# Layer 1 of a two-layer graph attention kernel: another order of the blocks per row, and of the steps that make the parts of the probabilities

## What is computed

```python
q, k, v = (split_heads(h @ W) for W in (Wq, Wk, Wv))
sim = jnp.einsum('bhid,bhjd->bhij', q, k) * scale
sim = jnp.where(adjacency_mask[:, None, :, :], sim, neg)
attn = jax.nn.softmax(sim, axis=-1)
out = jnp.einsum('bhij,bhjd->bhid', attn, v)
return out.transpose(0, 2, 1, 3).reshape(...) @ Wo + bo
```

## Time and profile before

| | |
|---|---|
| median of 3 runs | 2656.8 us |
| the profiled execution | 2656.29 us, span 2654.5 us |
| TensorE, matmuls busy | 2587.7 us (97%) |
| VectorE busy | 1990.9 us (75%) |
| ScalarE busy | 1754.5 us (66%) |
| GpSimd busy | 1399.6 us (53%) |
| mean granted TensorE clock | 0.994 |
| q, k and v blocks of layer 1, share of the chain that ended last | 19% |

### The profile page before, as it was taken

The page is one execution under the profiler, slowest core; times in us unless marked ns, Lnnn a source line. Parts: engine busy times, 40 slices in busy tenths (PEclk is TensorE's granted clock), DMA queues, the critical chain, the costliest instruction groups (busy, mean ns, idle before and its releaser), DMA issues. The chain is left out here.

```text
span 2654.5 us, 62516 instructions
## 1 busy us (share of the span) xinstructions
PE 2587.7 (97%) x20882; PEld 1393.6 (52%) x20886; DVE 1990.9 (75%) x6361; ACT 1754.5 (66%) x5020; POOL 1399.6 (53%) x2790
## 2 busy tenths in 40 slices
PE   6999999999999999999999999997999999999998
PEld 3455555555555555555555555554555555555554
DVE  6477778777877777777777777786777777777766
ACT  3566666666666666666666666675777777777774
POOL 4255545545554555555555555544565656555552
PEclk9999999999999999999999999998999999999999
DMA  5367766776667666766776677678786777778774
GB/s 141 61 136 158 144 135 133 149 155 130 145 141 140 145 128 144 149 142 133 141 147 141 131 140 146 148 141 195 158 175 160 169 163 170 164 160 170 158 149 102
DMA packets 945489, 387.43 MB, mean 146 GB/s; under 512 B 857617, under 2 KB 859153, under 8 KB 945169
## 3 DMA queue, kind: packets, MB, share of 16 engines
q1 hardware_dynamic: 945168, 383.44, 69.0%
HBM read 114.86 MB, written 67.11 MB: 69 GB/s over the span
## 5 line engine op out<-in xcount | busy, mean ns | idle before, releaser
L552 ACT ACTIVATE probs<-probs,negmax 128x128 f32<-128x128 f32 x1024 | 398.2, 390 | 455.6 <-DVE negmax L124 455.6
L465 POOL TENSOR_TENSOR o_sb<-o_sb,xres 128x512 f32<-128x512 f32 x127 | 161.5, 1272 | 496.5 <-DVE o_sb L739 493.1
L166 PE MATMUL l_ps_pj<-hT,room 128*128 128x512 f16 x1488 | 346.7, 383 | 2.3 <-ACT room L1343 2.3
L166 PE MATMUL ps_pj<-wm_hi,hT 128*128 128x512 f16 x1024 | 326.4, 380 | 12.6 <-DVE wm_lo L761 6.8
L166 PE MATMUL ps_pj<-wv_hi,hT 128*128 128x512 f16 x1024 | 326.4, 380 | 0.0
L166 PE MATMUL ps_pj<-hT,wk_hi 128*128 128x512 f16 x1024 | 305.9, 380 | 0.0
L166 PE MATMUL ps_pj<-hT,wq_hi 128*128 128x512 f16 x1024 | 304.5, 379 | 0.0
L1357 ACT ACTIVATE l_probs<-l_probs,l_negmax 128x128 f32<-128x128 f32 x512 | 199.2, 390 | 139.0 <-DVE l_negmax L124 138.8
L1292 POOL TENSOR_TENSOR l_h<-l_h 128x512 f16<-128x512 f32 x120 | 139.6, 1164 | 282.3 <-DVE l_out_sb L1440 245.0
L124 DVE CUSTOM_DVE_ANT_0 probs<-ps_sc,mask 128x128 f32<-128x128 f32 x1024 | 235.4, 285 | 47.4 <-PE ps_sc L981 46.7
L721 DVE SCALAR_TENSOR_TENSOR c<-cprobs,c 128x512 f16<-128x512 f32 x256 | 185.2, 723 | 79.6 <-ACT c L559 79.2
(11 more groups left out here) (172 smaller groups left out, 6198.8 us busy)
## 6 DMA issues: line engine op xcount, KB each, us to landing
xg<-in_x SPq DMA_DIRECT2D x128, 256.0 KB, 3.4
xres<-in_x SPq DMA_DIRECT2D x128, 256.0 KB, 3.1
x_scratch<-o_sb SPq DMA_DIRECT2D x128, 256.0 KB, 2.4
out<-l_out_sb SPq DMA_DIRECT2D x128, 256.0 KB, 3.3
l_ring<-x_scratch SPq DMA_DIRECT2D x124, 256.0 KB, 3.2
mask_u<-in_adj SPq DMA_DIRECT2D x64, 64.0 KB, 2.8
cpT<-c SPq DMA_TRANSPOSE x256, 3.2
xg<-x_scratch SPq DMA_DIRECT2D x12, 256.0 KB, 3.2
```

The costliest lines, as they stand in the source:

```text
L166: last = pe.matmul(out, a(kt), b(kt), start=(n == 0), stop=(n == 3 * kts - 1))
L465: nc.gpsimd.tensor_tensor(o_sb[:, j % 2], o_sb[:, j % 2], xres[:, j % 2], ALU.add).then_inc(res_done, 1)
L552: last = nc.scalar.activation(probs[:, i], probs[:, i], ACT.Exp, bias=negmax[:, u % 2, i:i + 1], scale=-1.0, accum_out=zsum[:, u % 4, hh:h ...
```

## The change

TensorE's order in an iteration becomes project_qk(n+4), project_v(n+4), project_out(n-4), scores(n+1), weigh_values(n-2). ScalarE and VectorE make the parts of the probabilities of row n at the start of iteration n, where before they made those of row n+1 at the end of it. On ScalarE v_high goes ahead of exps and behind relu and h_high; on VectorE v_low goes to the front, behind p_low. `normalise(n)` gets a wait for p_low(n-1), since it overwrites what that reads. At the start of the layer relu and h_high of rows 8 and 9 no longer stand behind p_high(0). The queues of GpSimd and SP stay as they are.

```diff
--- before.py
+++ after.py
@@ -1370,25 +1370,25 @@
                                      scale=1.0 / F16_SCALE).then_inc(ahi_done, 1)
 
             exps(0)
-            p_high(0)
             relu(MADE)
             h_high(MADE)
             relu(MADE + 1)
             h_high(MADE + 1)
             for n in range(B - QUAD):
                 qk_copy(n + QUAD)
+                p_high(n)
                 if n + 10 < B:
                     relu(n + 10)
                     h_high(n + 10)
+                v_high(n + QUAD)
                 exps(n + 1)
-                v_high(n + QUAD)
                 if n >= 2:
                     aT_high(n - 2)
-                p_high(n + 1)
             for n in range(B - QUAD, B - 1):
+                p_high(n)
                 exps(n + 1)
-                p_high(n + 1)
                 aT_high(n - 2)
+            p_high(B - 1)
             for i in range(B - 3, B):
                 aT_high(i)
 
@@ -1417,6 +1417,7 @@
 
             def normalise(n):
                 dve.wait_ge(exp_done, count(n + 1))
+                dve.wait_ge(plo_done, count(n))
                 nc.vector.reciprocal(rec[:], zsum[:, n % 2]).then_inc(rec_done, 1)
                 dve.wait_ge(rec_done, count(n + 1))
                 nc.vector.tensor_tensor(nprobs[:], probs[:], rec[:].unsqueeze(2).to_broadcast([P, HB, P]),
@@ -1442,28 +1443,28 @@
 
             row_max(0)
             normalise(0)
-            p_low(0)
             for i in range(HELD, 15):
                 stats(i)
             for n in range(B - QUAD):
+                p_low(n)
+                v_low(n + QUAD)
                 if n >= 4:
                     add_residual(n - 4)
                 row_max(n + 1)
                 if n + 15 < B:
                     stats(n + 15)
                 normalise(n + 1)
-                v_low(n + QUAD)
                 if n >= 2:
                     aT_low(n - 2)
-                p_low(n + 1)
             row_max(B - 3)
             for n in range(B - QUAD, B - 1):
+                p_low(n)
                 add_residual(n - 4)
                 normalise(n + 1)
                 if n + 2 < B:
                     row_max(n + 2)
-                p_low(n + 1)
                 aT_low(n - 2)
+            p_low(B - 1)
             for i in range(B - 5, B - 2):
                 add_residual(i)
                 aT_low(i + 2)
@@ -1534,10 +1535,10 @@
             scores(0)
             for n in range(B - QUAD):
                 project_qk(n + QUAD)
+                project_v(n + QUAD)
                 if n >= 4:
                     project_out(n - 4)
                 scores(n + 1)
-                project_v(n + QUAD)
                 if n >= 2:
                     weigh_values(n - 2)
             for n in range(B - QUAD, B - 1):
```

## The result

The changed kernel takes 2699.6 us (median of 4 runs, 2697.04 to 2703.99), 1.0168 times the kernel before (95% interval 1.0156 to 1.0181; before 2656.4 in the same comparison). The forecast was 2697.7. The profiled execution took 2697.04 us, span 2695.2; that is 40.7 us more span than before, where 41.4 had been forecast.

A forecast was written before the change was run, and what follows sets the result against it. TensorE bounds the kernel before at 6.51 us a row; afterwards a ScalarE-VectorE loop of 6.84 us does. 37.3 + 1.0 - 3.2 - 1.0 + 7.3 = 41.4 us on 2656.3 gives 2697.7 us, range 2677 to 2720.

The forecast's parts named there:

- a loop of ScalarE and VectorE: Layer 1's steady rows: v_low, waiting for v_high, delays the next maximum; this closed chain replaces TensorE's 6.51 us as bound.
- The loop's length: One row maximum to the next: seven start-to-start terms sum to 6.84 us, ends 6.75 and 6.95.
- up to row 5: Start of the layer: v_low's new place delays the first maxima, earlier q/k copies give most back; +1 us, bounds 0 and 3.
- rows 5 to 118, without the fourth trips' part: Steady part: 113 trips of the full loop, each 0.33 us longer; 37.3 us, bounds 27 and 50.
- every fourth multiply: Normalising multiply behind a group's factors: delayed 0.26 us by GpSimd's mask conversion, 28 times; 7.3 us, bounds 0 and 12.
- rows 118 to 124: After relu and h_high run out, the loop is 5.49 us and TensorE binds: 35.9 us instead of 39.1, so -3.2.
- row 124 to the end: Row 125's maximum no longer stands behind p_low and comes 1 us earlier, passed through to the end: -1.0 us.
- TensorE's two small waits a row: Steady stretch: TensorE waits for the q/k copy and for v_high, its share falling from 100% to about 95%.
- The parts one step later: p_high(n) still comes right after normalise(n) allows it; the weighing is two rows later: no cost.
- normalise's new wait: On VectorE, the wait for p_low(n-1) ends before the one for the exponentials does: no cost.
- rival (a): TensorE stays the bound and gains from its new block order, if the loop fits 6.5 us: 2644 us; chance 6%.
- The loop dearer by 0.5 us: Another delay, such as the multiply behind a bias addition, joins the loop in every trip: 2750 us; chance 8%.

The follow-up runs named there:

- both cuts of the loop: Changed kernel with the residual addition behind the row maximum: 2642.4 us; changed kernel with v_high ahead of relu and h_high: 2641.5 us.
- the two kernels with one instruction cut: Changed kernel with GpSimd's mask conversions from group 2 on cut to 8 columns: 2701.9 us; with every fourth row's bias addition cut to 64: 2692.6 us.
- the parts alone: Kernel before with only p_high(n) and p_low(n) moved to the start of iteration n, plus normalise's wait for p_low: 2652.5 us.
- both cures at once: Changed kernel with v_high ahead of relu and h_high and the residual addition behind the row maximum: 2638.9 us.
- TensorE's old order: Changed kernel with TensorE back to output, scores, then v; ScalarE and VectorE keep the new orders: 2721.0 us.
- TensorE's order alone: Kernel before with only the v block moved to directly behind q or k on TensorE: 2789.6 us.
- stats ahead of the maximum: Changed kernel with stats(n+15) moved ahead of the row maximum on VectorE, putting 0.82 us more into the loop: 2788.7 us.

## Why the prediction was right, point by point

**The bound changes from TensorE to a loop of ScalarE and VectorE.** Shown: both cuts of the loop bring TensorE's pace back, and lengthening it by 0.82 us brings 0.85.

**The loop's length.** Summed up to 6.84, measured 6.86 or 6.87. Term by term in the staircase above (forecast in brackets): maximum to p_high 3.58 (3.59), p_high 0.54 (0.53), relu to h_high 0.83 (0.83), h_high 0.52 (0.52), v_high to v_low 0.40 (0.38), v_low 0.34 (0.33), residual addition 0.66 (0.66). The last term, for which the trace of before had only the 0.76 of an addition followed by a waiting maximum, was rightly taken from the overlap.

**The span's 40.7 us**, from the starts of the maxima (the earlier trace rows for before: 1849.35 and 2623.93; row 118 of before at 2584.85):

| stretch | forecast | measured |
|---|---|---|
| up to row 5 | +1.0 | -0.1 |
| rows 5 to 118, without the fourth trips' part | +37.3 | +40.3 |
| every fourth multiply | +7.3 | +5.9 |
| rows 118 to 124 | -3.2 | -2.9 |
| row 124 to the end | -1.0 | -2.5 |
| sum | +41.4 | +40.7 |

113 trips took 781.7 us where before they took 735.5. The fourth trips are 0.21 us longer and 28 in number, 5.9 us; the rest, 40.3, is 113 x 0.36, where 0.33 was forecast: the loop was summed up some 0.025 us too short.

**The step that failed: which instruction the multiply meets.** The size (0.26 forecast, 0.21 measured) was near; the cause was wrong, and near by luck: the bias addition's end is as far past the multiply's due start (0.34 us) as the conversion's was thought to be (0.41). I had timed the factors by GpSimd's own queue and overlooked that they wait for the stats of the row (GpSimd waited 18.7 us in 28 cases for VectorE's L90). That the multiply ends 0.54 us after GpSimd's instruction held: 2246.83 to 2247.39 is 0.56. The Trainium skill, "SBUF — State Buffer", "Who interferes with whom", describes such an exclusive lock, taken by whichever instruction issues first; the two kernels with one instruction cut agree with it, and the residual addition, which reads PSUM, takes 0.74 us both beside an h_low (addition at 2236.11, h_low from 2235.54) and without one (2242.97).

**TensorE's two small waits a row.** Right in part. The weight loads wait for v_low in 51 rows and for the q/k copy in 25, but this is the smaller share of TensorE's idle time. Three quarters of it (33.3 of 44.5 us) is the wait of the scores for the q/k copy at the group starts, for which the forecast saw 1.4 us more time and no wait. It lies off the loop, so it cost the sum nothing. TensorE's share fell to 94% (95 forecast).

**The parts one step later cost nothing; normalise's new wait costs nothing.** Shown by the parts alone.

**The end.** The maximum of row 125 came 3.80 us after that of row 124, as worked out, where before it took 4.86. But only 0.5 us of this is left at row 127: the next distance grew from 3.58 to 4.18, since the multiply ahead of that maximum now takes 1.30 us where it took 0.69. Another 2.1 us came behind row 127, which no term of the forecast had. That the -1.0 was near the -2.5 is therefore no merit of its reasoning. The kernel with the parts alone has the same 2.1, but others with the same last steps have not; with both cures at once this stretch takes 15.6 us at full clock, with TensorE's old order 18.9 us, where the granted clock is 0.81. The cause stays open.

**The rivals.** That TensorE's new order saves time of its own was a part of rival (a), and is true: 6.40 in place of 6.51 us a row, seen as soon as the loop is out of the way (2642 where the rival had 2644). Only its condition, that the loop fits under TensorE's sum, did not hold. The loop dearer by 0.5 us did not come.

## What to carry to other kernels

Before moving steps between in-order queues, write down for each engine the cyclic order, and follow each chain of waits until it comes back to where it began; the longest closed chain, with start-to-start times from the timeline, is a floor under the time per row, however much idle time each engine has. When a queue is reordered, the dangerous place is an instruction that waits for another engine and now stands ahead of one that the third engine's next step needs: here v_low. A cure is to take out of the loop whatever doesn't need to be in it (a residual addition that nobody waits for soon), and a reordering that costs 1.7% can hide a gain of 0.5% that appears once the loop is cut.

## What the runs showed of the hardware

**Block order on TensorE has a price.** As recorded, a v block followed by the weighing takes 1.41 us to the next block's start, followed by the output block 1.31; the 0.21 us ahead of the weighing's weight loads is gone where scores precede it, and nothing replaces it. The Trainium skill, "TensorEngine Tiling (Array Packing)", "Key Properties", says that changing the tiling mode drains the engine. In the old order a row has four such changes (before and after the scores, before and after the weighing), in the new one three, since the two stand together. The number agrees with one change fewer, but no run isolates it; that scores and weighing, themselves of different modes (64 and 128 rows), show no gap between them isn't what the rule alone would give.

**Idle time under load does not always lower the clock.** All figures are for the stretch 1847 to 2586.5 us. In the changed kernel TensorE's matmuls are idle for 44.5 us in pieces of up to 1.3 us, and the granted clock stays at full speed (1.00). With TensorE's order alone they are idle for 100.2 us in pieces of up to 1.2 us, and it is 1.00 too. With TensorE's old order under the new ones they are idle for 44.6 us in pieces of up to 2.0 us, and it is 0.98; with stats ahead of the maximum for 93.0 us in pieces of up to 2.3 us, and it is 0.97. So here the total of the idle time doesn't tell whether the clock falls.
